# Row maxima masked on VectorE, eleven gate/up units and a table of PSUM banks in an attention and gated-FFN kernel

## The reference

```python
xn = (x - mean(x)) / sqrt(var(x) + 1e-5)
q, k, v = (xn @ W.T as 16 heads of 16 for W in (Wq, Wk, Wv))
att = q @ k.T / 4 + causal_mask          # 512 x 512 for each of 4 x 16 heads
s = softmax(att) @ v -> (4, 512, 256), then @ Wo.T
gate, up = silu(qlin(xn, wq_gate)), qlin(xn, wq_up)      # 704 hidden units
g = silu(qlin(gate * up, wq_down))       # qlin: int weights minus 128, times a row's scale
out = x + s * g
```

## Time and profile before

| | us |
|---|---|
| median of three timed runs | 327.85 |
| span of the profiled execution, first to last instruction | 323.8 |
| TensorE matmuls busy | 297.4 |
| VectorE busy | 184.7 |
| ScalarE busy | 173.6 |
| GpSimd busy | 142.4 |

### The profile page before, as it was taken

How to read it: one execution, slowest core, us unless ns; L and a number is a source line. 1 busy time by engine, 2 the same in 40 slices (tenths; PEclk the granted TensorE clock), 3 DMA queues, 4 the chain that set the end, 5 groups by cost and what they waited for, 6 DMA issues and landing times.

```text
span 323.8 us, 6058 instructions
## 1 busy us (share of the span) xinstructions
PE 297.4 (92%) x2352; PEld 206.7 (64%) x2352; DVE 184.7 (57%) x309; ACT 173.6 (54%) x251; POOL 142.4 (44%) x240
## 2 busy tenths in 40 slices
...
GB/s 279 275 138 200 195 145 67 5 69 127 173 90 156 43 3 130 15 122 72 177 147 169 29 68 2 18 120 66 180 141 172 27 69 3 2 2 67 69 0 67
DMA packets 21008, 31.56 MB, mean 97 GB/s; under 512 B 2148, under 2 KB 9956, under 8 KB 20980
## 3 DMA queue, kind: packets, MB, share of 16 engines
q1 hardware_dynamic: 20528, 30.50, 39.1%
...
## 4 chain that ended last, share of the span: by engine, by line
PE 67%; DMA 12%; SPq 5%; POOL 5%; issue 3%; DVE 3%; ACT 3%; ACTq 0%; POOLq 0%
PE ps L430 14%; PE ps L432 11%; PE ps L431 11%; PE ps L600 9%; PE ps L581 8%; DMA kp<-qk_scratch 7%; PE ps L540 7%; DMA sdb<-in_sd 4%; PE ps L552 4%; PE ps L608 2%; SPq L368 2%; POOL zbuf L901 1%; SPq L377 1%; SPq L370 1%; POOL hid L911 1%
## 5 line engine op out<-in xcount | busy, mean ns | idle before, releaser
L806 ACT ACTIVATE pt<-ps 128x1024 f32<-128x1024 f32 x80 | 81.8, 1027 | 36.0 <-PE ps L581 35.9
L949 POOL TENSOR_SCALAR_AFFINE_SELECT pt<-pt 128x256 f32<-128x256 f32 (+1 forms) x112 | 47.5, 439 | 94.8 <-ACT pt L806 94.1
L911 POOL TENSOR_TENSOR hid<-hid 128x512 f32<-128x512 f32 x24 | 31.3, 1302 | 55.9 <-ACT hid L748 36.2
L1080 DVE TENSOR_REDUCE mx<-ps 128x2 f32<-128x1024 f32 x32 | 39.1, 1224 | 20.2 <-PE ps L552 19.5
L540 PE MATMUL ps<-kp,qp 48*128 48x512 f32 (+3 forms) x256 | 36.2, 342 | 7.7 <-DVE mx L1080 3.1
L430 PE MATMUL ps<-xh,guh 128*128 128x512 f32 x96 | 42.2, 439 | 0.5 <-DVE u L1061 0.5
L600 PE MATMUL ps<-pt,vt 128*17 128x256 f32 (+3 forms) x512 | 42.2, 436 | 0.0
L581 PE MATMUL ps<-qp,kp 50*128 50x512 f32 (+3 forms) x256 | 39.6, 369 | 0.6 <-DMA qp<-ctr 0.3
L1085 DVE TENSOR_REDUCE mx<-ps 128x4 f32<-128x1024 f32 x16 | 19.6, 1226 | 35.0 <-PE ps L552 35.0
L1082 DVE TENSOR_REDUCE mx<-ps 128x2 f32<-128x768 f32 x32 | 30.6, 956 | 14.2 <-PE ps L552 14.1
L581 PEld LDWEIGHTS ps<-qp,kp 50*128 50x128 f32 x256 | 20.2, 184 | 28.8 <-issue 22.1
...
## 6 DMA issues: line engine op xcount, KB each, us to landing
...
```

The lines of the kernel that those rows point to most:

```text
L806: nc.scalar.activation(pt[:, 2 * kk:2 * kk + 2, :], ps[:, base:base + 2, :], ACT.Exp, scale=SCALE).then_inc(exp_done, 1)
L911: nc.gpsimd.tensor_tensor(a, a, hid[:, m % 2, 1, :], ALU.mult).then_inc(h_done, 1)
L949: mm = nc.gpsimd.affine_select(out=diag, in_=diag, compare_op=ALU.is_ge, fill=0.0, base=0, pattern=[[0, diag.shape[1]], [1, P]], channel_m ...
L1080: mm = nc.vector.tensor_reduce(mg[:, :, kk, 3], both, AX.X, ALU.max, negate=True)
```

## The change

- **Maxima.** The four mask matmuls of every `m` go. VectorE's reductions become `tensor_tensor_reduce`: scores plus a row `later` (0, and on the last 128 columns -1e38 above the diagonal), times -1, reduced with min, one call for each tile's run of values and each of the two banks: 16 calls a group for 7 reductions. Each call writes the sums back to PSUM, and builds as two instructions: the pass over the data, and one that writes the accumulator out.
- **Eleven gate/up units.** The last gate and up tiles (64 hidden units each) share one unit. Down's last tile holds high part and rest in one tile (new VectorE instruction `hidden_tail`, name `hst`), so it takes two matmuls for three; GpSimd has one `hlo` a block less.
- **PSUM.** All eight banks are one pool; a table gives every unit's bank or pair (`@` and number). `take` waits for the readers of whatever held it. exp's results have six pairs of slots for five.
- **pv** is one unit a group, after all five masks. The last block's z is no longer split in two halves.
- **Orders.** All six queues are written out as tables. The down and output weights are loaded after the first q and k, and prepared later.

```diff
-ST, MX, BZ, RING = 0, 2, 4, 5
...
+TENSOR = """
...
+m0.2@0 gu0.6@2 m0.3@4 gu0.7@3 v0.0@6 m0.4@0 gu0.8@7 v0.1@6 c0.0@2 m0.5@4 gu0.9@3 m0.6@0 gu0.10@2 s0.0@6 m0.7@4
...
+SYNC = """
+lx1.0 st0.0 st0.1 st0.2 lf0.0 lf0.1 ld0.0 ld0.1 ld0.2 st0.3 lx2.0 lr0.0 ld0.3 crow0.0 lwd0.0 lwo0.0 crow0.1
...
+def former_units():
+
+    out, held = {}, [None] * 8
+    for kind, b, n, bank in TENSOR:
+        if bank is None:
+            continue
+        mine = banks_of(kind, bank)
+        out[kind, b, n] = [u for u in dict.fromkeys(held[k] for k in mine) if u]
+        for k in mine:
+            held[k] = (kind, b, n)
+    return out
...
-            def take(unit):
+            def take(*unit):
...
+                for kind, b, n in BEFORE[unit]:
+                    if kind == "m":
+                        pe.wait_ge(max_done, STEPS * b + n + 1)
+                    elif kind == "s":
+                        pe.wait_ge(exp_done, STEPS * b + n + 1)
...
+                for m in range(HT - 1):
+                    split3(dst, hh[:, m, rows], hl[:, m, rows], wdh[:, m, :], wdl[:, m, :], m == 0, False)
+
+                nc.tensor.matmul(dst, hh[:, HT - 1, rows], wdh[:, HT - 1, :], start=False, stop=False)
+                nc.tensor.matmul(dst, hh[:, HT - 1, rows], wdl[:, HT - 1, :], start=False, stop=True).then_inc(f_ready, 1)
...
-                        mm = nc.tensor.matmul(dst, rows2[part, r, :], tri, start=False, stop=(r == 1))
+                        mm = nc.tensor.matmul(ps[:, base + e, c:c + w], qp[part, place(b, half), col, i * P:(i + 1) * P],
+                                              kp[part, place(b, half), col, 0:w], start=True, stop=True)
...
-                    nc.vector.tensor_reduce(mg[:, :, kk - 2, 2], both[:, :, 0:3 * P], AX.X, ALU.max, negate=True)
-                    mm = nc.vector.tensor_reduce(mg[:, :, kk - 2, 0], both[:, :, 3 * P:], AX.X, ALU.max, negate=True)
...
+                for e in range(2):
+                    for a, j, c in pair_blocks(kk, e):
+                        i = TT - 1 - j
+                        w, to = (i + 1) * P, 8 * e + 4 * (a // 2) + i
+                        part = ps[:, base + e, c:c + w]
+
+                        mm = nc.vector.tensor_tensor_reduce(part, part, later[:, T - w:], -1.0, HUGE, ALU.add, ALU.min,
+                                                            mx[:, n % 2, to:to + 1])
```

More of the change, by code:

```diff
@@ L157 @@
-HEAD_DONE |= {("c", 0, 0), ("ccp", 0, 0)} | {(k, b, i) for k in ("bn", "mom", "root", "xn") for b in range(2) for i in range(TT)}
-def entries(engine, steps, b, s):
-    first = FIRST[engine].get(s, []) if b == 0 else []
-    last = LAST[engine].get(s, []) if b == B - 1 else []
-    todo = [(kind, b + o, n) for kind, o, n in steps[s] if 0 <= b + o < B]
-    return [x for x in todo if x not in HEAD_DONE] + [(kind, b + o, n) for kind, o, n in first + last]
-def tail_units():
-    return [(kind, B - 1 + o, n) for kind, o, n in TAIL]
@@ L173 @@
-OWN_BANK = {("z2", B - 1, 1): ST, ("o", B - 1, 0): MX, ("o", B - 1, 1): MX + 1}
-IN_RING = [u for u in HEAD + [u for b in range(B) for s in range(STEPS) for u in entries("tensor", TENSOR_STEPS, b, s)]
-           + tail_units() if u[0] not in ("pv", "m", "s", "r") and u not in OWN_BANK]
-BANK = {u: RING + n % 3 for n, u in enumerate(IN_RING)}
-BANK.update(OWN_BANK)
-BEFORE = {u: IN_RING[n - 3] for n, u in enumerate(IN_RING) if n >= 3}
+TENSOR = """
+t0.0@0 t0.1@1 qk0.0@2 qk0.1@3 qk0.2@4 qk0.3@5 gu0.0@6 gu0.1@7 gu0.2@0 gu0.3@1 gu0.4@2 gu0.5@3 m0.0@4 m0.1@6
@@ new lines, with order, banks_of @@
+ld3.1 so1.1 ld3.2 st3.3 lr2.0 ld3.3 crow2.3 crow3.0 crow3.1 so2.0 crow3.2 so2.1 lr3.0 crow3.3 so3.0 so3.1
+"""
+def order(text):
+    out = []
+    for word in text.split():
+        name, _, bank = word.partition("@")
+        kind = name.rstrip("0123456789.")
+        b, _, n = name[len(kind):].partition(".")
+        out.append((kind, int(b), int(n), int(bank) if bank else None))
+    return out
+TENSOR, SCALAR, VECTOR, GPSIMD, SYNC = map(order, (TENSOR, SCALAR, VECTOR, GPSIMD, SYNC))
+def banks_of(kind, bank):
+    return (bank, bank + 1) if kind in ("m", "s") else (bank,)
@@ L182, in pair_blocks @@
+BANK = {(kind, b, n): bank for kind, b, n, bank in TENSOR if bank is not None}
+def former_units():
[7 more added lines that the diff above has]
+            held[k] = (kind, b, n)
+    return out
+BEFORE = former_units()
 def pair_blocks(kk, e):
@@ L469, in project_qk @@
             def project_qk(b, c):
-                bank = take(("qk", b, c))
+                bank = take("qk", b, c)
                 if c == 0:
@@ L482, in project_v @@
             def project_v(b, n):
[L483 to L485 removed]
+                bank = take("v", b, n)
+                if n == 0:
+                    pe.wait_ge(xlo_done, KD * (b + 1))
+                    if b == 0:
+                        pe.wait_ge(wl_done, 2)
                 for i in (2 * n, 2 * n + 1):
@@ L986, in root @@
                     nc.gpsimd.tensor_scalar(shf[:], t, -1.0, None, ALU.mult).then_inc(shf_done, 1)
[L988 to L999 removed]
+            work = {"root": root, "mask": mask, "hid": hidden, "hlo": hidden_lo, "res": residual, "oares": residual_first,
+                    "wds": shift_d, "wdc": scale_d}
+            for kind, b, n, _ in GPSIMD:
+                work[kind](b, n)
         @block.vector
```

874 lines of the change are left out of this document (340 added, 534 removed), and 20 rows, old and new, of the table TENSOR_STEPS.

## The result

The changed kernel takes 364.31 us (median of 4 runs, 363.94 to 365.05); the kernel before, on the same chip, 327.93 us. The ratio is 1.123, 95% interval 1.115 to 1.131: slower by 36 us, and 45 us above the predicted 319.5, outside its range.

What follows compares the result with a forecast made beforehand. TensorE's own work was taken as the bound, falling 6.9 us to 65 a block. s1.0 at 121.5, two blocks of 68 to 257.5, last block 58, end 315.5, plus 4.05: 319.5 us (range 304 to 334).

Steps and rivals of the forecast that it cites:

- TensorE's work, 65 us a block: Every block: TensorE's own work falls by 6.9 us, from 72.2 to 65 us.
- VectorE's price: Masked maxima on VectorE: 0.75 us for a 512-element call, 8.75 us a group for 6.4; VectorE 53 us a block.
- rival in which the maxima become the chain: VectorE's maxima bound the kernel: 329 to 350 us and over, above 350 at two cycles an element; chance 0.18.
- Blocks 1 and 2, 68 us: Steady blocks, s1.0 to s3.0: 65 us of TensorE work plus 3.4 us of waits, 68 us a block for 72.2.
- m2.0 0.8 for k's load: Steady blocks: the first score-maximum unit of block 2 waits 0.8 us for the load of k.
- Head, s0.0 at 45.2: Start up to block 0's first score unit: it starts at 45.2 us, 4 us sooner than before.
- I leave m0.0 at 30: Head: the first unit for the maxima stays at 30 us, now behind six gate/up units.
- c0.0 at 40.5: Head: the first c unit, after VectorE's maxima and shift, starts at 40.5 us, 3 us sooner than 43.74.
- Block 0, 76.3: s0.0 to s1.0: TensorE stands 13 us for maxima, dn0.0 starts at 68, s1.0 at 121.5 us as before.
- later wd and wo: Block 0: loading and preparing down and output weights later costs nothing, hidden by the wait for maxima.
- rival that short waits halve the clock: TensorE's clock drops behind short waits: 3.2 us a block, 10 us at most, likely 325 us; chance 0.14.
- Last block, 58: s3.0 to the end: last c 34 us in, then 4.4, 5.5, 0.6, 2.35 and 13; 58 us, as before.

Runs made afterwards that it cites:

- g1: The changed kernel, all orders kept, with q and k stores and loads moving only 256 of 512 columns from block 2 on: 337.5 us, ratio 1.036.
- b2: The kernel before with only the masked maxima: mask matmuls gone, VectorE's reductions become the masked calls; 318.6 us, ratio 0.974.
- b3: b2 plus the eleven gate/up units with their hst, orders and banks as in the kernel before: 318.0 us, ratio 0.977.
- b6: b3 with only half the columns of q and k stored and loaded from block 2 on: 314.5 us, ratio 0.964.
- e3: The changed kernel with the next block's t and qk units ahead of dn, four stores ahead of the loads, banks chosen anew: 347.9 us, ratio 1.074.
- b1: The kernel before with only SyncE's loop rearranged, stores and loads of q and k interleaved like the changed kernel: 341.0 us, ratio 1.045.
- e2: e1 with the head reordered: st0.2 behind the first four loads back, x2's load later, shift0.0 ahead of bn2.0; 372.4 us, ratio 1.143.
- e5: e3 with the head mended: weights loaded first, two stores, loads of x2, x3 and residual, and their statistics later; 344.9 us, ratio 1.060.
- f2: e5 with the preparation of down's and the output projection's weights moved from block 0's maxima into the head: 339.8 us, ratio 1.043.
- b4: The kernel before with the mask matmuls left out and VectorE's reductions unchanged: 317.1 us, ratio 0.976.
- e1: The changed kernel with only SyncE's list rearranged, the next block's four q and k stores together ahead of the loads: 374.1 us, ratio 1.147.
- e4: e1 with q and k stores and loads moving only 256 of 512 columns from block 2 on: 340.3 us, ratio 1.048.
- f1: f2 with block 0 reordered, qk1, pv0.0 and dn0.0 units between the maxima, x2's statistics and loads later, banks anew: 339.7 us, ratio 1.046.

## Why the prediction was wrong, step by step

- **TensorE's work, 65 us a block: right.** g1 runs 65.9 and 65.2 at full clock. By parts, as means of the two steady blocks: 72.3 before; 2.3 less by the mask (b2; 3.3 in the block where the faster TensorE meets little of the read-back, forecast 3.8); 1.1 by the twelfth unit (b3; forecast 1.9); 1.3 of read-back that the old order had by then (b6); 2.1 by orders, banks and `pv` (forecast 1.2 for `pv` and changes). The total fits better than its parts.
- **VectorE's price: wrong, on the safe side.** 7.2 us a group for 8.75, 212 us in all for 225 to 235. The rival in which the maxima become the chain did not happen, though the time lies where it put "above 350". A time near a rival's does not show the rival's mechanism; its rows do.
- **Blocks 1 and 2, 68 us: the failed step.** The prediction followed the new orders of TensorE and VectorE and took the read-back as one wait, "m2.0 0.8 for k's load". It never laid SyncE's list and ScalarE's waits on `qk_stored` beside them. The blocks take 78.3 us. The change leaves 24 us for a path that had 32, in a kernel where m2.0 already waited 0.21 us for k. Shown by g1 (bytes halved, 65.5), e3 (more room, 72.2) and b1 (the list alone, 341 us in the old kernel).
- **Head, s0.0 at 45.2: wrong by 14.0.** "I leave m0.0 at 30" cost 5.1, most of it by st0.2 ahead of the loads (e2 gives 31.9). c0.0 at 40.5 came at 50.0: another 4.4, by `bn2.0` ahead of the shift behind x2's load; without it c0.0 comes 9.3 us behind m0.0 (e2), for the 10.5 forecast, so VectorE's list itself was priced too long and not too short. c0.0 to s0.0, taken as 4.7, took 9.2, since c's rows share the DMA engines with loads that the old order did not have there.
- **Block 0, 76.3: wrong by 11.8.** The stand of TensorE from maxima was foreseen. Not foreseen: "later wd and wo" costed at nothing. Moved among the maxima, GpSimd's instruction lengthens the shift by 3.5 of the 4.3 us that dn0.0 is late; away from there, with the preparation of wo and wd, block 0 is 6.9 us shorter (e5 to f2). The other 7.5 us lie behind dn0.0: the 6.49 at s0.16 are the read-back again, and e3 takes 3.0 off the block.
- **Clock.** The rival that short waits halve the clock was real as an addition: 0.93 and 0.94 in the steady blocks, 0.83 in block 0, 1.00 in g1's steady blocks. It priced 3.2 us a block; some 4 come on top of the 8.5 us of waits. Not every wait has it: b4's steady block with the wait of 1.89 us stays at 1.00.
- **Last block, 58: right in the sum only, by luck.** It takes 58.8, but its own terms (34, 4.4, 5.5, 0.6, 2.35 and 13) add up to 59.9. The last `c` comes at 31.8 for 34, the part behind it takes 27.0 for 25.9, with `pv` at 4.5 us for 2.35 at the lower clock. In e1 and e4, whose last block is the same, it takes 55.1 and 55.2 us, with a clock of 0.96 for 0.81.
- The parts without the orders are the better kernel: b2 and b3 take 318 us, 2.3 to 2.6% less than before and 13% less than the changed kernel.
- **Left open:** 3.6 us of block 0 in f2 over the forecast, what f1 would take without its wait for k, and what sets the clock of the last block.
